# Both layer norms and the residual sum of three token chunks computed inside the attention stage

## The chip, the cores and the metric

The kernel runs on one core of a Trainium2 chip. The time is device microseconds of one execution of the whole program; several executions give a median. A core has a matrix engine (PE, TensorE; its weight loads are listed as PEld), a vector engine (DVE, VectorE), a scalar engine (ACT, ScalarE), GpSimd (POOL) and SP, which here only issues DMAs. Each engine runs its own instruction list in order and waits on semaphores that the others count up.

## The reference, cut to what matters

The model is four layers over 8 sequences of 256 tokens with 256 features (2048 tokens, held as 16 tiles of 128 tokens). The part that the change touches:

```python
x = L0_attn_hidden_states
x = x + _layernorm(_L0_attn_ref(_layernorm(x), w_qkv, b_qkv, w_proj, b_proj))   # y = the attention's output
rows = _layernorm(x)                                                            # what the experts read
x = x + _layernorm(_L0_ffn_ref(rows, router_w, ...))                            # 64 experts, 4 per token
...                                                                             # a scan layer, a feed-forward layer

def _layernorm(x, axis=-1, eps=1e-05):
    m = jnp.mean(x, axis=axis, keepdims=True)
    v = jnp.var(x, axis=axis, keepdims=True)
    return (x - m) / jnp.sqrt(v + eps)
```

Attention has 16 heads of 16 features, a causal mask and a linear position bias. The router computes 64 logits for each token from `rows`, takes the best four experts, and each token's row is written into a slot of each of its four experts.

## The kernel before

The program is a row of stages with a barrier between them. Two matter here.

**Attention** (`stage_attention`, some 82 to 225 us of the span) goes over 16 *units*; a unit is 8 heads of one sequence, so two units make a sequence. All engines loop over a head counter `i`; head `i` lies in unit `i // 8`. For each head PE computes the scores of the head 16 places further on (L529, L530, into one of three banks `ps`) for the maxima that DVE takes (`maxima`, L636 and L638), and then the turned scores of the head itself (L541 to L546, into one of two banks `pst`), of which ACT takes the exponential (`weigh`, L615). The third bank rule is what couples DVE to PE: PE may write scores `n` only once the maxima of `n - 3` are out. The second couples ACT: PE may write turned scores `n` only once the exponential of `n - 2` is out. At the second head of every unit (`i % 8 == 1`) PE does three more things in this order: `turn` (L573), which needs the maxima of a whole unit; `values` (L560), the product with the values of the unit before; and in even units from the fourth on `project` (L583) for a whole sequence. ACT hands the turned maxima over (`hand_over`, L609), POOL splits them into three short rows (L510 to L513), SP writes these into the stack that the turned scores of the next unit but one loop step read (`place`, L484). DVE inverts the sums and normalises (L647, L651), and in even units adds the projection's bias (`add`, L656): that is `y`. In units 4 to 10 SP also issues one block of zeros each (1 MB of `slots_in`, from `blank`, L2617); 16 blocks are needed in all before tokens may be scattered.

**Routing** (`stage_route`, 225 to 381 us) takes the statistics of `y` (`statistics`, L1020 to L1031 on DVE; one over the deviation on POOL, `deviations`, L813 and L814), scales `y` on ACT (L955), adds it to `x` on DVE (`add`, L1036), takes the statistics of `x`, and lets ACT write the normalised `rows` (L955), in four chunks of four tiles. PE turns `rows` (L855), ACT and DVE keep high and low parts (L960, L1042), PE computes the router's logits (`score`, L869), DVE chooses four experts for each token (`choose`, L1048 to L1057), PE counts and ranks (L876 to L887), DVE works out the slot numbers (`tables`, `find_slots`, L1069 to L1121), and POOL scatters the rows with 64 indirect DMAs, 16 for each chunk (L842). POOL also splits the weights of the shared expert (`split`, L819 and L822), and after the scores PE, ACT and DVE run the shared expert's eight steps (L917, L1002, L1137, L1006, L1141) for the first two chunks. The stage ends when the last scatter has landed and the last product of that expert is stored (L995). The other nine blocks of zeros are issued at its start.

Of the kernel before, what the change touches and what calls it, by code (L numbers as in the profile page):

```python
# [13 lines left out]
P = 128  # L14
# [401 lines left out]
LAST_ADD = (UNITS + 2) * HALF + AT_ADD  # L416

# [12 lines left out]
FILL_FIRST, FILL_AT = 7, 4  # L430


def stage_attention(chip, vpad, qk_dram, stack, consts, y, ident, fill, ins):
# [9 lines left out]
    with ExitStack() as ctx:  # L443
# [23 lines left out]
        projected, y_ready = chip.sem("projected"), chip.sem("y_ready")  # L467

# [3 lines left out]
        with nc.Block() as block:  # L472
# [25 lines left out]
            def _(pool):  # L498
# [7 lines left out]
                for u in range(UNITS):  # L506
                    pool.wait_ge(shift_out, u + 1)
                    if u:
# [5 lines left out]
                                            ).then_inc(max_split, 1)  # L514

# [88 lines left out]
            def _(act):  # L604
# [13 lines left out]
                for i in range(-LEAD * HALF, STEPS + HALF):  # L618
                    n = i + LEAD * HALF
                    if 0 <= i < STEPS:  # L620
                        weigh(i)
                    if n % HALF == AT_BLOCK and 0 < n // HALF <= UNITS:
                        hand_over(n // HALF - 1)

            @block.vector
            def _(dve):
# [32 lines left out]

                dve.wait_ge(loaded, 6 * 16)  # L660
# [18 lines left out]
NORM_ORDER = [(0, 0), (0, 1), (1, 0), (1, 1), (0, 2), (0, 3), (1, 2), (1, 3)]  # L679
# [17 lines left out]
def stage_moe(chip, front, spare, x, xh, xl, y, ident, xs, xs_clear, fill, ys, t, ins):  # L697
    with ExitStack() as room:
        sb, _ = chip.memory(room)
        rows = sb("rows", [P, NT, D])  # L700
        stage_route(chip, x, rows, xh, xl, y, ident, xs, xs_clear, fill, t, ins)
# [7 lines left out]
def stage_route(chip, x, rows, xh, xl, y, ident, xs, xs_clear, fill, t, ins):  # L709
# [10 lines left out]
    with ExitStack() as ctx:  # L720
# [25 lines left out]
        stats = sb("stats", [P, 2, NT, 6])  # L746
        small = sb("small", [P, 5, TPC])
        power = sb("power", [P, TPC])
        negmean, var, rstd, shift = (sb(n, [P, 2, NT]) for n in ("negmean", "var", "rstd", "shift"))
# [23 lines left out]
        var_ready, rstd_ready, y_scaled = chip.sem("var_ready"), chip.sem("rstd_ready"), chip.sem("y_scaled")  # L773
# [16 lines left out]
        def normed(kind, g):  # L790
            return NORM_ORDER.index((kind, g)) + 1

        with nc.Block() as block:
# [10 lines left out]
            def _(pool):  # L804
# [3 lines left out]
                link(nc.gpsimd.memset(power[:], -0.5))  # L808
                pool.wait_ge(none_set, 1)

                def deviations(kind, g):
                    pool.wait_ge(var_ready, normed(kind, g))
                    link(nc.gpsimd.tensor_tensor(rstd[:, kind, tiles(g)], var[:, kind, tiles(g)], power[:], ALU.pow))  # L813
                    nc.gpsimd.tensor_tensor(shift[:, kind, tiles(g)], negmean[:, kind, tiles(g)],  # L814
                                            rstd[:, kind, tiles(g)], ALU.mult).then_inc(rstd_ready, 1)
# [9 lines left out]
                for g in range(2):  # L825
                    deviations(OF_Y, g)
                for g in range(2):
                    deviations(OF_X, g)
                for g in range(2, NCH):
                    deviations(OF_Y, g)  # L830
                split(0)
                deviations(OF_X, 2)
                split(1)
                deviations(OF_X, 3)
                split(2)
                split(3)
# [10 lines left out]
            def _(pe):  # L847
                def turn(g):
                    for b in (2 * g, 2 * g + 1):
                        pe.wait_ge(xn_ready, b + 1)  # L850
# [46 lines left out]

                pe.wait_ge(split_done, 2)
                turn(0)
# [5 lines left out]
                place_chunk(1)  # L905
                turn(3)
                score(2)
# [45 lines left out]
            def _(act):  # L953
                def scaled(dst, src, kind, i):
# [60 lines left out]
            def _(dve):  # L1015
# [128 lines left out]
                for g in range(2):  # L1144
                    statistics(y, OF_Y, g)
# [1606 lines left out]
```

## Time and profile before

| | |
|---|---|
| time of three executions | 1388.35, 1390.89, 1393.96 us; median 1390.89 |
| span of the profiled execution | 1388.8 us (its own device time is not listed apart; the median lies 2.1 us above the span) |
| busy share of the span | PE 84%, PEld 70%, DVE 62%, ACT 45%, POOL 27% |
| attention | 82.0 to 225.1 us |
| routing | 225.1 to 381.5 us; first scatter at 277.0, last begun at 366.2 |

The profile is of one execution. A row of a timeline gives the start, the length, the engine, the line, the written and the read tiles with their shapes, and a count when several equal instructions are merged; the bracket is the idle time of the engine ahead of it and what released it. Times of different engines can be laid side by side, since all are counted from the span's start. The granted clock of TensorE is 1.00 (2.4 GHz) through the middle of attention and about 0.5 (1.2 GHz) through the first half of routing.

### The profile page before, as it was taken

The numbers are of one execution on the slowest core, as the hardware profiler recorded it, in microseconds if no ns is written. First come the engines' busy times: TensorE is split into PE (matmuls) and PEld (weight loads), VectorE is DVE, ScalarE is ACT, GpSimd is POOL, SyncE is SP. The second block draws the span as 40 slices with busy tenths as digits, with TensorE's granted clock in tenths as the row PEclk, the third lists the DMA queues.
The fourth block names the chain that finished last, engine by engine and source line by source line (L and its number), as shares of the span: only waits on it lengthen the run. The fifth ranks groups of instructions, "written<-read, shape, count | busy, mean of one in ns | idle before, by whom it ended". The sixth has DMA issues, their size and how long they took to land. (4 is left out here: it accounts for less than half of the span.)

```text
span 1388.8 us, 25315 instructions
## 1 busy us (share of the span) xinstructions
PE 1168.4 (84%) x9088; PEld 974.9 (70%) x9088; DVE 863.8 (62%) x2165; ACT 618.7 (45%) x1415; POOL 370.3 (27%) x467
## 2 busy tenths in 40 slices
PE   6669994635689998767779999999999999997886
PEld 5537762634588986545648888888888888886775
DVE  6468876945546665577456666566666666663464
ACT  5434543302133443446644554545455445552564
POOL 3321112576400446572024005001400240000110
PEclk9879997556789998877799999999999999999998
DMA  7725724322199874353243233223342332222001
GB/s 172 182 78 159 229 66 164 161 103 83 57 397 417 290 254 138 91 155 122 89 113 108 82 94 122 77 84 99 115 137 85 107 107 80 81 62 80 1 16 46
DMA packets 77529, 177.21 MB, mean 128 GB/s; under 512 B 12566, under 2 KB 26134, under 8 KB 74710
## 3 DMA queue, kind: packets, MB, share of 16 engines
q1 hardware_dynamic: 71132, 158.54, 34.7%
q0 software_dynamic: 6272, 17.05, 4.0%
q8 instruction: 73, 1.20, 0.3%
q14 instruction: 52, 0.43, 0.1%
HBM read 114.26 MB, written 61.08 MB: 126 GB/s over the span
## 5 line engine op out<-in xcount | busy, mean ns | idle before, releaser
L2195 ACT ACTIVATE decay<-masked,negcum 128x128 f32<-128x128 f32 x512 | 164.1, 391 | 240.7 <-issue 156.1
L2300 DVE COPY cT<-pcT 128x512 f32<-128x512 f32 x128 | 88.4, 690 | 175.7 <-PE pcT L2119 175.7
L2130 PEld LDWEIGHTS pcb<-cT,bT 128*128 128x128 f32 x1024 | 134.4, 191 | 10.6
L2130 PE MATMUL pcb<-cT,bT 128*128 128x128 f32 x1024 | 135.3, 275 | 0.0
L2057 POOL TENSOR_TENSOR wh<-wraw,none 128x512 fp32r<-128x512 f32 x32 | 34.2, 1070 | 318.9 <-DMA wraw<-in_w_bc 225.4
L2119 PE MATMUL pbT<-xh,wh 128*128 128x512 f32 x256 | 111.9, 437 | 1.3 <-POOL wl L2060 1.3
L2259 DVE TENSOR_TENSOR mixT<-pcb,decay 128x512 f32<-128x512 f32 x128 | 88.5, 691 | 22.9 <-PE pcb L2130 22.6
L2119 PE MATMUL pcT<-xh,wl 128*128 128x512 f32 x256 | 100.6, 393 | 0.0
L2119 PE MATMUL pbT<-xl,wh 128*128 128x512 f32 x256 | 100.1, 391 | 0.0
L2119 PE MATMUL pbT<-xh,wl 128*128 128x512 f32 x256 | 100.0, 390 | 0.0
L2119 PE MATMUL pcT<-xh,wh 128*128 128x512 f32 x256 | 99.7, 390 | 0.0
L2119 PE MATMUL pcT<-xl,wh 128*128 128x512 f32 x256 | 99.6, 389 | 0.0
L2249 DVE TENSOR_TENSOR masked<-cumrow,mask 128x512 f32<-128x512 f32 x128 | 94.1, 736 | 0.0
L615 ACT ACTIVATE probT<-pst 128x384 f32<-128x384 f32 x128 | 60.0, 490 | 68.0 <-PE pst L546 65.3
L2214 ACT ACTIVATE bT<-pbT 128x512 f32<-128x512 f32 x128 | 74.2, 580 | 25.7 <-PE pbT L2119 25.6
L1506 POOL DMA_INDIRECT back<-slots_out,slots x64 | 68.0, 1062 | 28.5 <-issue 28.0
L842 POOL DMA_INDIRECT slots_in<-rows,slots x64 | 65.4, 1022 | 34.0 <-issue 18.9
L1372 DVE TENSOR_TENSOR hT<-gate,pgu 64x512 f32<-64x512 f32 x64 | 44.2, 691 | 31.0 <-ACT gate L1347 30.6
L1240 POOL COPY copies<-weights 128x384 f32 x64 | 32.4, 507 | 114.7 <-issue 95.6
L2119 PEld LDWEIGHTS pbT<-xh,wh 128*128 128x128 f32 x256 | 48.4, 189 | 12.0 <-issue 4.8
L2268 DVE TENSOR_TENSOR cS<-cT,grown 128x256 f32<-128x256 f32 x128 | 56.8, 444 | 0.1
L2119 PEld LDWEIGHTS pbT<-xh,wl 128*128 128x128 f32 x256 | 48.1, 188 | 10.9
(387 smaller groups left out, 3020.1 us busy)
## 6 DMA issues: line engine op xcount, KB each, us to landing
cumrow<-ssm_cum SPq DMA_DIRECT2D x128, 256.0 KB, 3.2
slots_in<-blank SPq DMA_DIRECT2D x16, 1024.0 KB, 10.6
xg<-slots_in SPq DMA_DIRECT2D x32, 512.0 KB, 6.3
slots_out<-spare SPq DMA_DIRECT2D x32, 512.0 KB, 3.8
weights<-in_expert_quads SPq DMA_DIRECT2D x16, 768.0 KB, 10.1
wraw<-in_w_bc SPq DMA_DIRECT2D x32, 256.0 KB, 3.7
qk_parts<-parts SPq DMA_DIRECT2D x32, 192.0 KB, 2.3
stack<-qk_parts SPq DMA_DIRECT2D x32, 192.0 KB, 3.4
```

The costliest lines, as they stand in the source:

```text
L615: nc.scalar.activation(probT[:, n % HELD, :], pst[n % T_BANKS][:, 0:3 * P], ACT.Exp).then_inc(exped, 1)
L842: nc.gpsimd.indirect_dma_start(out=xs[:, :], out_offset=bass.IndirectOffsetOnAxis(slots[:, i, k:k + 1], 0), in_=rows[:, i, :], in_offset=N ...
L1372: last = nc.vector.tensor_tensor(hT[k * FE:(k + 1) * FE, g % 2, :], gate[FE:P, g % 2, :], pgu[g % 2][FE:P, :], ALU.mult)
L1506: nc.gpsimd.indirect_dma_start(out=back[:, i % BACK, k, :], out_offset=None, in_=ys[:, :], in_offset=bass.IndirectOffsetOnAxis(slots[:, i, ...
L2119: last = nc.tensor.matmul(bank[:], w[:, j, col:col + P], a[:, k, c * CHUNK:(c + 1) * CHUNK], start=(m == 0), stop=(m == len(parts) - 1))
L2130: last = nc.tensor.matmul(pcb[n % 2][:, o], bT[:, n % 2, o], cT[:, n % 2, o], start=True, stop=True)
L2195: last = nc.scalar.activation(decay[:, n % 2, o], masked[:, n % 2, o], ACT.Exp, bias=negcum[:, c * TPC + i, head:head + 1])
L2214: nc.scalar.activation(bT[:, n % 2, :], pbT[:], ACT.Copy).then_inc(b_out, 1)
L2249: nc.vector.tensor_tensor(masked[:, n % 2, :].rearrange("p (i l) -> p i l", l=P), cumrow[:, n % CUMS, :].rearrange("p (i l) -> p i l", l=P ...
L2259: nc.vector.tensor_tensor(mixT[:, n % KEEP, :], pcb[n % 2][:], decay[:, n % 2, :], ALU.mult).then_inc(mix_out, 1)
L2268: nc.vector.tensor_tensor(cS[:, n % KEEP, :, :], second, grown[:, n % 2, :, :], ALU.mult).then_inc(c_scaled, 1)
L2300: nc.vector.tensor_copy(cT[:, n % 2, :], pcT[:]).then_inc(c_out, 1)
```

## The change

Of the first three chunks (tiles 0 to 11), the whole of norm, residual sum and second norm is done inside attention, some units after the chunk's `y` is there. Only the last chunk (tiles 12 to 15) stays in the routing stage; of it the statistics of the first two tiles of `y` are taken in attention too. The formulas of the statistics use `bn_aggr` for each tile in place of five small operations for each four tiles. In the attention stage the residual sum runs on POOL, one 128x1024 addition for each chunk. Twelve blocks of zeros are issued in units 4 to 15 in place of seven in units 4 to 10, four instead of nine in routing. In routing PE scores chunk 2 before it turns chunk 3, and DVE chooses for chunk 2 before the low parts of chunk 3. `rows` and the small norm tiles are allocated ahead of attention.

```diff
+EARLY_NORMS = 3
+NORM_SCALE, NORM_SUM, NORM_ROWS = 7, 8, 9
+def measure(nc, link, norms, kind, tiles):
+    for i in tiles:
+        last = nc.vector.bn_aggr(moments[:, kind, i, :], norms["stats"][:, kind, i, :])
+    link(last)
+    nc.vector.tensor_scalar(norms["negmean"][:, kind, part], moments[:, kind, part, 0], -1.0, None, ALU.mult)
+    return nc.vector.tensor_scalar(norms["var"][:, kind, part], moments[:, kind, part, 1], EPS, None, ALU.add)
+def spread(nc, link, norms, kind, tiles):
+    link(nc.gpsimd.tensor_tensor(rstd, norms["var"][:, kind, part], norms["power"][:], ALU.pow))
+    return nc.gpsimd.tensor_tensor(norms["shift"][:, kind, part], norms["negmean"][:, kind, part], rstd, ALU.mult)
+def normal(nc, norms, dst, src, kind, i):
+    return nc.scalar.activation(dst, src, ACT.Identity, bias=norms["shift"][:, kind, i:i + 1],
+                                scale=norms["rstd"][:, kind, i:i + 1])
-FILL_FIRST, FILL_AT = 7, 4
+FILL_FIRST, FILL_AT = 12, 4
@@ attention, gpsimd
-                for u in range(UNITS):
+                for u in range(UNITS + 2):
+                    if u < UNITS:
+                        split(u)
+                    g, at = (u - NORM_SCALE) // 4, (u - NORM_SCALE) % 4
+                    if 0 <= g < EARLY_NORMS and at == 0:
+                        pool.wait_ge(y_measured, g + 1)
+                        spread(nc, norm_step, norms, OF_Y, tiles(g)).then_inc(y_spread, 1)
+                    if 0 <= g < EARLY_NORMS and at == NORM_SUM - NORM_SCALE:
+                        residual(g)          # x = x + y, waits for y_scaled
+                    if 0 <= g < EARLY_NORMS and at == NORM_ROWS - NORM_SCALE:
+                        pool.wait_ge(x_measured, g + 1)
+                        spread(nc, norm_step, norms, OF_X, tiles(g)).then_inc(x_spread, 1)
@@ attention, scalar
+                    g, at = (i // HALF - NORM_SCALE) // 4, (i // HALF - NORM_SCALE) % 4
+                    if 0 <= g < EARLY_NORMS and at == 0 and 2 <= i % HALF < 2 + TPC:
+                        scale_y(g, g * TPC + i % HALF - 2)
+                    if 0 <= g < EARLY_NORMS and at == NORM_ROWS - NORM_SCALE and i % HALF >= HALF - TPC:
+                        fill_row(g, g * TPC + i % HALF - (HALF - TPC))
@@ attention, vector
+                    seq = i // HALF // 2 - 2
+                    if i % (2 * HALF) == AT_ADD + 2 and 0 <= seq < B - 1:
+                        y_statistics(seq)    # two bn_stats; with an odd seq also measure()
+                    g = (i + 1) // HALF // 4 - 2
+                    if 0 <= g < EARLY_NORMS and (i + 1) % (4 * HALF) in (HALF, HALF + 1):
+                        x_statistics(g, (i + 1) % HALF)   # two bn_stats each; the second also measure()
                     u = i // HALF - 2
                     if i % HALF == AT_BLOCK and 0 <= u < UNITS:
@@ routing, vector
-                for g in range(2):
-                    statistics(y, OF_Y, g)
+                statistics(y, OF_Y, last_tiles[TPC // 2:])
...
-                for g in range(2):
-                    add(g)
-                    statistics(x, OF_X, g)
                 set_tables()
-                statistics(y, OF_Y, 2)
                 low_parts(0)
-                statistics(y, OF_Y, 3)
                 low_parts(1)
-                add(2)
-                statistics(x, OF_X, 2)
                 choose(0)
-                add(3)
-                statistics(x, OF_X, 3)
+                add()
+                statistics(x, OF_X, last_tiles)
                 choose(1)
                 low_parts(2)
                 tables(0)
                 find_slots(0)
                 find_slots(1)
+                choose(2)
                 low_parts(3)
-                choose(2)
                 choose(3)
@@ routing, scalar
-                scale_y(0)
-                scale_y(1)
-                normal(0)
                 high_parts(0)
-                normal(1)
-                scale_y(2)
+                scale_y()
                 high_parts(1)
-                scale_y(3)
-                normal(2)
                 high_parts(2)
-                normal(3)
+                fill_rows()
                 high_parts(3)
```

**DVE, units 8 and 9.** DVE's list where the maxima of heads 86 to 88 (loop steps 70 to 72) stand; `ps` are the score banks, `norm_stats` and `norm_moments` the new small tiles. Before, and then after:

```order
L636 ISA masked,highest<-ps_74,reach 128x128
L636 ISA highest 128x1
L638 ISA masked,highest<-ps_74,reach 128x256
L638 ISA highest 128x1
L636 ISA masked,highest<-ps_75,reach 128x128
L636 ISA highest 128x1
L638 ISA masked,highest<-ps_75,reach 128x256
L638 ISA highest 128x1
```

```order
L737 BN_STATS norm_stats<-y 128x6 x2
L708 ISA masked,highest<-ps_74,reach 128x128
L708 ISA highest 128x1
L710 ISA masked,highest<-ps_74,reach 128x256
L710 ISA highest 128x1
L745 BN_STATS norm_stats<-x 128x6 x2
L708 ISA masked,highest<-ps_75,reach 128x128
L708 ISA highest 128x1
L710 ISA masked,highest<-ps_75,reach 128x256
L710 ISA highest 128x1
L745 BN_STATS norm_stats<-x 128x6 x2
L427 BN_AGGR norm_moments<-norm_stats 128x2 x4
```

Three groups of statistics stand between the maxima of three heads that followed one another, the last with four `bn_aggr` and two small scalings behind it.

**DVE, the end of attention.** The last rows ahead of the barrier (`y` of sequences 6 and 7, `rinv` and `oT` of the last unit). Before, and then after:

```order
L656 TENSOR_TENSOR y<-misc,bproj 128x512
L647 RECIPROCAL rinv<-po_80 128x128 x2
L651 TENSOR_TENSOR oT<-po_80,rinv 128x256
L656 TENSOR_TENSOR y<-misc,bproj 128x512
L472 UNCONDITIONAL_BRANCH
```

```order
L728 TENSOR_TENSOR y<-misc,bproj 128x512
L737 BN_STATS norm_stats<-y 128x6 x2
L745 BN_STATS norm_stats<-x 128x6 x4
L427 BN_AGGR norm_moments<-norm_stats 128x2 x4
L430 TENSOR_SCALAR norm_negmean<-norm_moments 128x4
L431 TENSOR_SCALAR norm_var<-norm_moments 128x4
L719 RECIPROCAL rinv<-po_80 128x128 x2
L723 TENSOR_TENSOR oT<-po_80,rinv 128x256
L728 TENSOR_TENSOR y<-misc,bproj 128x512
```

The statistics of two tiles of `y` and of all four tiles of chunk 2 of `x` now stand ahead of the last unit's reciprocals, on which the last projection waits.

**ACT, unit 7.** ACT's list from the handing over of the maxima (`shift`) on; `probT` are the exponentials. Before, and then after:

```order
L609 ACTIVATE shift<-misc 16x128
L615 ACTIVATE probT<-pst_77 128x384
L615 ACTIVATE probT<-pst_78 128x384
L615 ACTIVATE probT<-pst_77 128x384
L615 ACTIVATE probT<-pst_78 128x384
L615 ACTIVATE probT<-pst_77 128x384
```

```order
L666 ACTIVATE shift<-misc 16x128
L672 ACTIVATE probT<-pst_77 128x384
L444 ACTIVATE y<-y,norm_shift,norm_rstd 128x256
L672 ACTIVATE probT<-pst_78 128x384
L444 ACTIVATE y<-y,norm_shift,norm_rstd 128x256
L672 ACTIVATE probT<-pst_77 128x384
L444 ACTIVATE y<-y,norm_shift,norm_rstd 128x256
L672 ACTIVATE probT<-pst_78 128x384
L444 ACTIVATE y<-y,norm_shift,norm_rstd 128x256
```

Four scalings of a tile now alternate with four exponentials.

## Rows read from the trace of the kernel before

**Rows 1.** Busy time of each engine in attention; then the DMA queue of 220:277 (packets, MB, share).

```profile
82.00:225.13 143.13, 132.05 (x1854) 95.43 (x1852) 107.36 (x538) 62.48 (x144) 22.34 (x64) 0.95 0.41 121
...
q1 hardware_dynamic: 2016, 11.24, 50.4%
```

**Rows 2.** Timeline (start, us, engine, line, out<-in, [idle before <-releaser]), ACT, attention.

```profile
129.86 3.02 ACT L615 ACTIVATE probT<-pst 128x384 f32<-128x384 f32 x6 [2.86 <-PE pst L546]
```

**Rows 3.** Timeline, DVE, 123.8 to 129.6, attention.

```profile
123.85 0.69 DVE L656 TENSOR_TENSOR y<-misc,bproj 128x512 f32<-128x512 f32 x1
...
125.56 0.28 DVE L636 CUSTOM_DVE_ANT_0 masked<-ps,reach 128x128 f32<-128x128 f32 x1
...
129.58 0.29 DVE L636 CUSTOM_DVE_ANT_0 masked<-ps,reach 128x128 f32<-128x128 f32 x1
```

**Rows 4.** Timeline, PE, the same two units.

```profile
126.25 0.28 PE L573 MATMUL misc<-ident,highest 128*16 128x128 f32 x1
...
130.70 0.22 PE L529 MATMUL ps<-stack 99*128 99x128 bf16 x1
...
132.58 0.27 PE L541 MATMUL pst<-stack 102*128 102x256 bf16 x1
```

**Rows 5.** Timeline, POOL and then SP's queue, the same unit.

```profile
127.06 0.28 POOL L510 CAST short<-shift 16x128 bf16<-16x128 f32 x1 [7.50 <-ACT shift L609]
...
128.71 2.62 SPq L484 DMA_DIRECT2D stack<-short  x3
```

**Rows 6.** Timeline, DVE, the end of attention.

```profile
218.04 0.69 DVE L656 TENSOR_TENSOR y<-misc,bproj 128x512 f32<-128x512 f32 x1 [5.90 <-PE misc L583]
218.65 1.76 DVE L647 RECIPROCAL rinv<-po 128x128 f32<-128x128 f32 x2
```

**Rows 7.** Timeline of the routing stage: DVE, POOL, DVE, ACT.

```profile
225.46 1.41 DVE L1020 BATCH_NORM_STATS2 stats<-y 128x6 f32<-128x256 f32 x4 [0.32 <-PEq L472]
...
228.06 1.01 POOL L813 TENSOR_TENSOR rstd<-var,power 128x4 f32<-128x4 f32 x1 [2.36 <-DVE var L1031]
...
230.12 0.22 DVE L1147 CAST wh<-wraw 128x128 fp32r<-128x128 f32 x1
...
237.54 2.07 ACT L955 ACTIVATE rows<-x,shift,rstd 128x256 f32<-128x256 f32 x4 [3.86 <-POOL shift L814]
```

**Rows 8.** Timeline, PE and then DVE, scores of chunks 0 and 1.

```profile
244.20 0.40 PE L869 MATMUL pu<-wh,xh 128*128 128x64 f32 x1
...
254.44 1.11 PE L855 MATMUL acc<-ident,rows 128*128 128x128 f32 x4
...
259.63 0.42 DVE L1048 TENSOR_TENSOR ranked<-pg,bias 128x256 f32<-128x256 f32 x1
```

**Rows 9.** Timeline, POOL beside DVE, twice.

```profile
246.37 1.47 POOL L819 TENSOR_TENSOR sh<-sraw,none 128x768 fp32r<-128x768 f32 x1
...
246.47 0.68 DVE L1042 TENSOR_TENSOR xl<-acc,xh 128x512 fp32r<-128x512 f32 x1
...
265.98 1.81 POOL L822 TENSOR_TENSOR sl<-sraw,sh 128x768 fp32r<-128x768 f32 x1
...
266.12 1.72 DVE L1074 TENSOR_SCALAR tiles_i<-count_i 128x64 int32<-128x64 int32 x1
```

**Rows 10.** Timeline of the scatter: POOL, then DVE, then ACT.

```profile
276.99 1.22 POOL L842 DMA_INDIRECT slots_in<-rows,slots  x1 [9.20 <-DVE slots L1121]
...
323.56 0.96 POOL L842 DMA_INDIRECT slots_in<-rows,slots  x1 [5.88 <-DVE slots L1121]
...
366.22 0.96 POOL L842 DMA_INDIRECT slots_in<-rows,slots  x1 [0.30 <-issue]
...
304.49 0.22 DVE L1069 TENSOR_TENSOR table<-table,counts 128x64 f32<-128x64 f32 x1 [14.78 <-remote]
...
319.89 0.60 ACT L1002 ACTIVATE gate<-pg 128x512 f32<-128x512 f32 x1 [52.41 <-remote]
...
380.14 1.09 ACT L995 ACTIVATE y<-acc 128x512 f32<-128x512 f32 x2 [3.26 <-PE acc L927]
```

More of the change, by code:

```diff
@@ L616, in weigh, with scale_y, fill_row @@
                                          ).then_inc(exped, 1)
-                for i in range(-LEAD * HALF, STEPS + HALF):
+                def scale_y(g, i):
+                    act.wait_ge(y_spread, g + 1)
+                    last = normal(nc, norms, y[:, i, :], y[:, i, :], OF_Y, i)
+                    if i % TPC == TPC - 1:
+                        last.then_inc(y_scaled, 1)
+                def fill_row(g, i):
+                    act.wait_ge(x_spread, g + 1)
+                    normal(nc, norms, rows[:, i, :], x[:, i, :], OF_X, i)
+                for i in range(-LEAD * HALF, STEPS + 2 * HALF):
                     n = i + LEAD * HALF
@@ L658, in add, with y_statistics, x_statistics @@
                                             ).then_inc(y_ready, 1)
+                link = linker(dve, norm_chain)
+                def y_statistics(seq):
+                    dve.wait_ge(y_ready, seq + 1)
+                    for i in (2 * seq, 2 * seq + 1):
+                        last = nc.vector.bn_stats(norms["stats"][:, OF_Y, i, :], y[:, i, :])
+                    link(last)
+                    if seq % 2 and seq // 2 < EARLY_NORMS:
+                        measure(nc, link, norms, OF_Y, tiles(seq // 2)).then_inc(y_measured, 1)
+                def x_statistics(g, half):
+                    dve.wait_ge(x_added, g + 1)
+                    for i in tiles(g)[2 * half:2 * half + 2]:
+                        last = nc.vector.bn_stats(norms["stats"][:, OF_X, i, :], x[:, i, :])
+                    link(last)
+                    if half:
+                        measure(nc, link, norms, OF_X, tiles(g)).then_inc(x_measured, 1)
                 dve.wait_ge(loaded, 6 * 16)
@@ L694, with stage_moe @@
 I32 = mybir.dt.int32
[L697 to L701, printed above, removed]
+def stage_moe(chip, front, normed, spare, x, rows, norms, xh, xl, y, ident, xs, xs_clear, fill, ys, t, ins):
+    stage_route(chip, x, rows, norms, xh, xl, y, ident, xs, xs_clear, fill, t, ins)
+    normed.close()
     front.close()
@@ L953, in _ @@
             def _(act):
-                def scaled(dst, src, kind, i):
-                    return nc.scalar.activation(dst, src, ACT.Identity, bias=shift[:, kind, i:i + 1],
-                                                scale=rstd[:, kind, i:i + 1])
                 def high_part(b):
```

118 lines of the change are left out of this document (59 added, 59 removed).

## The prediction

> **What bounds the kernel now.** I read the page's slices, then busy time by stretch, then the timelines of the stages that the change touches. Work leaves the start of routing and enters attention, so I ask of each whether it has room.
>
> Attention has little. PE is busy 132 of 143 us at clock 0.95 [rows 1]. ACT takes six exponentials back to back, 3.02 us or 0.50 each, and idles only ahead of them, 2.86 us, while PE does `values` [rows 2]; in between PE waits for ACT, since there are two banks. DVE takes a head's maxima in 0.555 us. From 125.56, where head 7's begin, it does 7, 8 and 9, then two reciprocals and `oT`, and is at the next head at 129.58: no hole [rows 3]. I call the heads of the even unit shown 0 to 7 and those of the odd unit behind it 8 to 15. PE's turn at 126.25 needs the maxima of head 7, out at 125.56 + 0.56 = 126.12: slack 0.13. PE's scores of head 13 at 130.70 need head 10's maxima, out at 129.58 + 0.56 = 130.14: slack 0.56 [rows 3, 4]. POOL's split begins at 127.06, SP's writes 1.65 later, and the turned scores of the next unit begin at 132.58, 3.87 after SP started [rows 4, 5]; the gap ahead of those scores says that this chain sets them in odd units. Even units have the projection's 2 us as slack.
>
> Routing up to the scatter is one chain through the norms: scores of chunk 0 start at 244.20, 19.1 us after the stage's begin S (225.13), the scatter at 276.99, S + 51.9 [rows 8, 10].
>
> **Attention, part by part.** Prices: a `bn_stats` 0.35 (1.41 for 4), a scaling on ACT 0.52 (2.07 for 4), POOL's `rstd` 1.01, with its `shift` 1.25 [rows 7]. `bn_aggr` is not in the trace. `measure` is four of them and two scalings, against seven small operations that took, with the handing over to POOL, 2.60 - 1.41 = 1.19 us [rows 7]. Below, six pipelined at 0.08 give 0.5; above, aggregates as dear as `bn_stats` give 1.65. I take 0.65, nearest to the small ones.
>
> *Two `bn_stats` of y behind head 6 of an even unit.* Maxima 7 come 0.74 later, slack 0.13: PE's turn and all behind it +0.6. With `measure` (odd sequences) +1.25. Unit 4: 0.6. Units 6 and 10: 1.25 each. Unit 14: nothing, since its maxima are over and DVE waits.
>
> *Four scalings between exponentials, units 7, 11, 15.* ACT is full there, so 4 x 0.52 = 2.0 each, 6.0 in all. The idle 2.86 us can't cover them, because they stand behind heads 2 to 5.
>
> *Units 8 and 9, and 12 and 13.* Statistics behind head 6 (0.74), 7 (0.74) and 8 (0.74 + 0.65). Head 7's maxima are out at 126.87, the turn +0.65. Head 8's end at 128.17, `x_measured` comes at 129.6, head 9's at 130.1, reciprocals and `oT` 132.4, head 10's maxima at 133.0, where PE wanted them at about 131.3: +1.65, +2.3 in all, and PE then goes at DVE's 0.555 and at ACT, which has four `rows` among these heads; `values` would begin 2.9 late. The POOL chain is later still: POOL waits in its list for `x_measured`, so `spread` ends at 130.95, the split that was due at 127.7 ends at 132.6, and 3.87 behind it, at 136.5, PE gets its rows, 3.9 after 132.58. I take 3.8 for each pair of units, 7.6. Behind the waiting POOL instruction stands only this split; it is PE that waits for it.
>
> *The end.* The six `bn_stats` and `measure` stand ahead of the reciprocals that followed the add at once, 218.04 to 218.65 [rows 6]. The last projection waits for these: 6 x 0.35 + 0.1 + 0.65 = 2.85. Chunk 2's four `rows` on ACT lie beside it.
>
> Sum: 0.6 + 2.5 + 6.0 + 7.6 + 2.85 = 19.55 us. With dear aggregates five `measure` on the path add 5; if the stretches overlap better (ACT's delays lying over DVE's), I don't get below 12. So 12 to 25.
>
> *At nothing.* POOL's residual sum is 1.81 x 1024/768 = 2.4 us [rows 9], three times; it waits for ACT's last scaling and ends about when the next split is due, in an even unit. Does it stop DVE? Beside POOL's 1.47 us operation DVE's `xl`, which reads one operand from PSUM, took 0.68 [rows 9], as the add of 512 columns did with POOL idle (0.69, [rows 3]); the maxima read `ps` in the same way: no. The five more blocks of zeros (units 11 to 15) run where little else is loaded; each stands on SP ahead of a `place` that comes a unit later.
>
> **Routing up to the scatter.** `rows` of chunks 0 to 2 are there at S. PE turns chunk 0 at once. Chunk 1 and the scores wait for the split router weights; the cast began at S + 5.0 without a wait [rows 7], so its load was in by then, I take S + 4. Then come two memsets, the tables and four low parts, of which chunk 0's end at S + 6.5, and chunk 1's turning in PE's list holds the scores to S + 7.0. Gain there 19.1 - 7.0 = 12.1. Two chunks of scores take 254.44 - 244.20 = 10.24 [rows 8], until S + 17.3. DVE chose chunk 1 at 259.63, 5.2 behind the scores' end, because the sum and the statistics of chunk 3 lay between [rows 8]; now these follow `choose(0)` and end at S + 18.55, 1.3 behind it: 3.9 more, 16.0.
>
> Against it: three of POOL's four splits now follow the last `spread` (S + 19.8) and run to S + 30, over `tables(0)`, which starts at S + 22.6. DVE is slow beside them: a 64-column operation took 1.72 us, until POOL's of 265.98 ended [rows 9], where one of that width takes 0.22 [rows 10]. One or two slip in between two of POOL's, so I put DVE at a quarter of its pace: over 7.4 us that loses 5.3. Before, the splits ended at 267.8 [rows 9], some 4 us into the tables, and cost about 3: -2. Gain 14.0, scatter at S + 37.9. Bounds: no contention 17, standing still throughout and `measure` dear 11.
>
> The Trainium skill ("SBUF — State Buffer", SBUF: two separate sides) says that the port pair of VectorE and GpSimd is an exclusive lock for the whole instruction, against a VectorE operation with two SBUF inputs or a two-port mode. By that rule DVE would do nothing in the 7.4 us, and the gain would be 12 instead of 14; the trace shows it slipping an operation in between POOL's, so the sum goes by the trace.
>
> The nine blocks of zeros were 9 of the 11.24 MB that kept the queue at 50.4% of 57 us [rows 1], 2.6 us for a MB; four and the shared weights take 14 us, done by S + 17. They bound nothing before (scatter at S + 51.9) and nothing now.
>
> Up to the scatter: +19.55 - 14.0 = +5.5.
>
> **From the scatter on.** The first 32 indirect DMAs run 41 us, POOL then waits 5.88, and the rest ends at 367.2; the stage's last copies end at 381.2, 104.3 after the first scatter [rows 10]. In that time DVE stood 14.78 us and ACT 52.41, both behind PE's signals that by PE's rows were due at 291 and 293, and ACT went on at 319.89 just when the scatter paused [rows 10]. I can't name the cause, and the change doesn't touch it: DVE's and ACT's last work ahead of it stands 13 to 16 us into the scatter as before. I take 104.3 unchanged.
>
> Total: +5.5 on 1390.9, **1396 us**. The sum is made on the profiled span of 1388.8; I set its difference on the median, 2.1 above.
>
> **Rivals.**
> *A, as summed,* 1396; attention's +12 to +25 and the gain of 17 to 11 give bounds of 1386 to 1405. Chance 42%.
> *B, faster: the hold beside the scatter shrinks.* It could, since choosing for chunk 2 now comes earlier and the pause of 5.88 goes when slots are ready. Then only POOL's 64 operations bound it: 90.2 less 5.88, and 2 for landing, 86 in place of 104.3, up to 18 less: 1378; half of it 1387. For it: the PE part ahead ends earlier; against it: two engines were held to the pause, whatever lay ready. 30%.
> *C, slower: the hold lasts longer.* If ACT is freed only when POOL pauses, and DVE has chunk 2's slots ready before that, POOL goes on with 48 instead of 32, 1.27 us each, 20 us more; ACT's eight steps, 61 us from 319.89, then start that much later: +18, 1414, decided by whether slots of chunk 2 are ready before the 32nd DMA. Against it: in the trace DVE was held too. 17%.
> *D, attention costs only 10* because ACT's insertions and DVE's lie over one another: 1387. For it: while ACT holds PE, DVE catches up; against: only units 7 and 8 touch, and the turn waits for DVE before it. 11%.
>
> **How the numbers follow.** About 0.5%, 7 us, can be told from no change: faster is below 1384, slower above 1398. A gives same 27, slower 15; B faster 20, same 10; C slower 17; D faster 4, same 7. So faster 0.24, same 0.44, slower 0.32. The range 1380 to 1411 takes in A, D, most of B and C up to 1411; A's own is 1386 to 1405.
>
> **What would show it.** Attention should last 155 to 168 instead of 143 us; in units 7, 11 and 15 PE waits for ACT over four heads; in units 9 and 13 the turned scores wait for `stack<-short`, some 4 us; the last reciprocals come 3 us behind the add. The scatter should begin 36 to 41 us after the stage's start, and the stage end some 104 us after that. Wrong: attention growing by under 10, or the scatter-to-end stretch shifted by over 8 us.

## The result, and the profile after

The changed kernel took 1402.6 us (median of 7 runs, 1395.9 to 1410.3) against 1391.7 for the kernel before, beside which it ran: ratio 1.0071, 95% interval 1.0049 to 1.0094, so 0.7% slower, some 10 us by the ratio and 11 by the medians. The forecast was 1396, in the range 1380 to 1411. The profiled execution has a span of 1399.5 us against 1388.8.

I cut both traces at the same three places: ScalarE's first copy of `shift`, the start S of the routing stage, and the stage's last copy of `y`. First the busy times of attention's whole, then of stretches of it (us, busy us of PE, PEld, DVE, ACT and POOL, PEclk, DMA share, GB/s), and then the DMA queue of the routing stage up to the scatter:

```profile
86.00:251.92 165.92, 141.06 (x1853) 99.93 (x1852) 121.04 (x598) 73.42 (x168) 36.33 (x79) 0.90 0.42 136
...
178.00:187.00 9.00, 7.44 (x93) 5.62 (x83) 6.46 (x38) 3.80 (x8) 1.41 (x4) 1.00 0.81 271
187.00:190.50 3.50, 3.50 (x41) 2.15 (x45) 3.09 (x11) 0.27 (x1) 1.94 (x6) 0.53 0.51 209
...
214.70:221.20 6.50, 5.75 (x59) 3.31 (x61) 3.11 (x11) 2.74 (x7) 1.40 (x4) 0.50 0.41 166
...
246.00:251.50 5.50, 3.78 (x8) 2.52 (x8) 1.59 (x4) 2.07 (x4) 0.53 (x2) 0.50 0.00 0
...
q1 hardware_dynamic: 1296, 6.00, 36.8%
```

Attention has as many matmuls as in [rows 1], but they are busy 9 us longer, and the granted clock is 0.90 for 0.95. Both kernels enter the stage at the lower of TensorE's two levels, 1.2 GHz (until 91.6 us before and 98.4 after; up to unit 4 the difference in time is 0.3 us). Behind that the changed kernel ran at the lower level in four stretches; three of them stand here, the fourth is 235 to 238.5. The timeline of PE (start, us, line, out<-in, wait and releaser) shows the first of them and the last, and then the last projection of the kernel before:

```profile
186.93 0.28 PE L630 MATMUL misc<-ident,highest 128*16 128x128 f32 x1 [1.27 <-DVE highest L710]
187.13 1.08 PE L617 MATMUL po<-probT,vpad 128*32 128x256 f32 x8
...
247.41 3.78 PE L640 MATMUL misc<-wproj,oT 128*128 128x256 f32 x8 [5.97 <-DVE oT L723]
...
220.92 3.49 PE L583 MATMUL misc<-wproj,oT 128*128 128x256 f32 x8 [2.92 <-DVE oT L651]
```

The turn waited 1.27 us for VectorE's maxima, and the eight matmuls of `values` behind it took 1.08 us; in a unit at 2.4 GHz the same row says 0.64. The last projection waited 5.97 us and took 3.78; the ones before it took 1.99. The kernel before had its last projection slow too, 3.49 us behind a wait of 2.92: that was its only stretch at 1.2 GHz between 91.6 us and the end of attention. So the changed kernel's longer wait costs 3 us there, and the clock only 0.3 more than before. Why it waited stands in VectorE's timeline, which answers to [rows 6]:

```profile
241.48 0.69 DVE L728 TENSOR_TENSOR y<-misc,bproj 128x512 f32<-128x512 f32 x1 [8.85 <-PE misc L640]
242.21 0.75 DVE L737 BATCH_NORM_STATS2 norm_stats<-y 128x6 f32<-128x256 f32 x2
243.00 1.54 DVE L745 BATCH_NORM_STATS2 norm_stats<-x 128x6 f32<-128x256 f32 x4
244.57 0.38 DVE L427 BATCH_NORM_AGGREGATE norm_moments<-norm_stats 128x2 f32<-128x6 f32 x4
244.99 0.17 DVE L430 TENSOR_SCALAR norm_negmean<-norm_moments 128x4 f32<-128x4 f32 x1
245.06 0.16 DVE L431 TENSOR_SCALAR norm_var<-norm_moments 128x4 f32<-128x4 f32 x1
245.13 1.76 DVE L719 RECIPROCAL rinv<-po 128x128 f32<-128x128 f32 x2
```

From the add to the reciprocals it is 3.65 us, 0.61 before. In the routing stage (S = 251.92) VectorE and GpSimd answer to [rows 9], first DVE's, then POOL's:

```profile
277.17 1.72 DVE L1134 TENSOR_SCALAR tiles_i<-count_i 128x64 int32<-128x64 int32 x1
278.92 1.39 DVE L1135 TENSOR_SCALAR table<-tiles_i 128x64 f32<-128x64 int32 x1
280.35 1.84 DVE L1136 TENSOR_SCALAR table<-table 128x64 f32<-128x64 f32 x1
...
277.03 1.81 POOL L907 TENSOR_TENSOR sl<-sraw,sh 128x768 fp32r<-128x768 f32 x1
278.80 1.47 POOL L904 TENSOR_TENSOR sh<-sraw,none 128x768 fp32r<-128x768 f32 x1
280.34 1.80 POOL L907 TENSOR_TENSOR sl<-sraw,sh 128x768 fp32r<-128x768 f32 x1
```

Each of these DVE operations begins just behind or with a POOL operation and ends with it, within 0.05 us. The scatter, as in [rows 10] POOL, DVE and then ACT:

```profile
290.88 1.22 POOL L920 DMA_INDIRECT slots_in<-rows,slots  x1 [8.74 <-DVE slots L1181]
...
337.98 0.96 POOL L920 DMA_INDIRECT slots_in<-rows,slots  x1 [6.58 <-DVE slots L1181]
...
380.94 0.96 POOL L920 DMA_INDIRECT slots_in<-rows,slots  x1 [0.30 <-issue]
...
324.25 0.22 DVE L1129 TENSOR_TENSOR table<-table,counts 128x64 f32<-128x64 f32 x1 [17.73 <-remote]
...
336.18 0.60 ACT L1071 ACTIVATE gate<-pg 128x512 f32<-128x512 f32 x1 [53.80 <-remote]
...
394.24 1.08 ACT L1064 ACTIVATE y<-acc 128x512 f32<-128x512 f32 x2 [2.51 <-PE acc L1006]
```

| | before | after | difference | forecast |
|---|---|---|---|---|
| first `shift` copy | 82.75 | 86.47 | +3.7 | 0 |
| attention, from there to S | 142.4 | 165.5 | +23.1 | +19.55 |
| S to the first scatter | 51.9 | 39.0 | -12.9 | -14.0 |
| first scatter to the last copy's end | 104.2 | 104.4 | +0.2 | 0 |
| the rest | 1007.6 | 1004.2 | -3.4 | 0 |

The first and the last line are not the change's: with the same code ahead of attention the first `shift` copy came between 81.6 and 86.5 us in the traces below (86.34 in e1, whose kernel is the one before but for five transfers in attention), so the trace of before was an early one. In the twelve traces whose T stands in the next table the rest lasted between 998 and 1014 us, with the same code.

### The profile page after: what moved, and what is told of

Same layout as the page of the kernel before. It is cut to its first block and busy times, and to the rows that moved or that the text cites. A ratio compares the mean times of both kernels' runs of the same rounds, so it can differ in the third digit from the quotient of the medians.

```text
span 1399.5 us, 25308 instructions
## 1 busy us (share of the span) xinstructions
PE 1170.5 (84%) x9088; PEld 974.1 (70%) x9088; DVE 857.9 (61%) x2154; ACT 617.8 (44%) x1415; POOL 376.8 (27%) x470
## 5 line engine op out<-in xcount | busy, mean ns | idle before, releaser
L2311 DVE TENSOR_TENSOR mixT<-pcb,decay 128x512 f32<-128x512 f32 x128 | 88.5, 692 | 22.9 <-PE pcb L2182 22.6
L920 POOL DMA_INDIRECT slots_in<-rows,slots x64 | 65.5, 1024 | 34.2 <-issue 18.9
L1424 DVE TENSOR_TENSOR hT<-gate,pgu 64x512 f32<-64x512 f32 x64 | 44.2, 691 | 30.6 <-ACT gate L1399 30.2
```

Of the source, the lines that this page charges most:

```text
L920: nc.gpsimd.indirect_dma_start(out=xs[:, :], out_offset=bass.IndirectOffsetOnAxis(slots[:, i, k:k + 1], 0), in_=rows[:, i, :], in_offset=N ...
L1424: last = nc.vector.tensor_tensor(hT[k * FE:(k + 1) * FE, g % 2, :], gate[FE:P, g % 2, :], pgu[g % 2][FE:P, :], ALU.mult)
L2311: nc.vector.tensor_tensor(mixT[:, n % KEEP, :], pcb[n % 2][:], decay[:, n % 2, :], ALU.mult).then_inc(mix_out, 1)
```

## The experiments

The ratios are to the kernel before in the same series, with 95% intervals. Attention (A), S to the first scatter (R) and the first scatter to the last copy (T) are read from each run's trace in the way above.

| run | A | R | T | ratio |
|---|---|---|---|---|
| before | 142.4 | 51.9 | 104.2 | 1 |
| after | 165.5 | 39.0 | 104.4 | 1.0071 (1.0049 to 1.0094) |
| e1_fill | 142.5 | 51.9 | 109.4 | 1.0006 (0.9991 to 1.0021) |
| e2_act | 157.1 | 39.0 | 106.6 | 1.0047 (1.0030 to 1.0064) |
| e3_dve | 148.7 | 38.8 | 111.0 | 0.9967 (0.9951 to 0.9984) |
| e4_both | 143.9 | 38.9 | 105.4 | 0.9930 (0.9910 to 0.9950) |
| e5_busy | 159.6 | 38.0 | 103.8 | 1.0001 (0.9977 to 1.0024) |
| e6_tail | 139.8 | 38.8 | 103.8 | 0.9899 (0.9861 to 0.9938) |
| e7_tiny | 166.3 | 33.3 | 105.8 | 1.0044 (1.0016 to 1.0072) |
| e8_order | 167.1 | 39.5 | 105.1 | 1.0068 (1.0041 to 1.0095) |
| e9_final_2 | 139.3 | 34.5 | see below | 0.9865 (0.9841 to 0.9889) |
| e10_before_tail_2 | 139.0 | 51.9 | see below | 0.9982 (0.9966 to 0.9997) |
| e11_after_2 | 168.1 | 39.1 | 105.0 | 1.0088 (1.0053 to 1.0122) |
| e12_final_again_2 | 139.5 | 35.2 | 107.1 | 0.9861 (0.9839 to 0.9883) |

T swings by 7 us with nothing changed in it, so one trace's span tells little. A repeats within 0.5 us where the granted clock does (139.8, 139.3 and 139.5 in e6, e9 and e12). R lay between 38.0 and 39.1 with the changed kernel's code for it, and at 34.5 and 35.2 with e9's.

**e1_fill.** The kernel before with the blocks alone:
```diff
-FILL_FIRST, FILL_AT = 7, 4
+FILL_FIRST, FILL_AT = 12, 4
```


> The kernel before with FILL_FIRST at 12: the five more blocks of slots are zeroed in attention and nothing else is changed. Theory (these 5 writes lie in DMA queues that the attention stage leaves half idle): the ratio to the kernel before is 1.000 within 0.002, attention 142.4 us within 0.3, and the routing stage 156.4 within 0.5. Rival (they push the stack loads or the three shift rows back): attention grows by 1 to 3 us, ratio above 1.001. Beside this, a profile of it tells how far the front stage, whose code is the same in all kernels, moves from execution to execution: its first shift copy came at 82.75 us before and at 86.47 after.


A 142.5, R 51.9, ratio 1.0006. The five blocks cost nothing and bring nothing. The routing stage took 161 us, where 156.4 within 0.5 was expected: all of it is T, 5.2 longer in this trace, and the ratio does not show it.

**e2_act.** ScalarE's scalings and fills behind a `shift` copy, four at a time:
```diff
-if ... at == 0 and 2 <= i % HALF < 2 + TPC:
-    scale_y(g, g * TPC + i % HALF - 2)
+if i % HALF == AT_BLOCK:      # units 7, 11, 15; rows in 10, 14 and behind the last
+    for k in tiles(g): scale_y(g, k)
```


> The changed kernel with ScalarE's twelve scalings of y and twelve fills of rows taken from between the exponentials and put, four at a time, right behind a shift copy, where ScalarE idles 2.6 us (y, units 7, 11 and 15) or 4.6 us (rows, units 10 and 14, and behind the last unit). VectorE and GpSimd as in the changed kernel. Theory (each group of four between exponentials held TensorE 2.0 us, and the granted clock fell once more behind it): attention 165.5 - 6.0 - up to 3 = 156 to 159.5 us, total 1393 to 1397, ratio to the kernel before 1.001 to 1.004. Rival (the excess over my sum, 3.5 us, comes from VectorE's statistics alone): attention only 6 us shorter at most, TensorE still at 1.2 GHz behind the turn of units 11 and 15. Second rival (contention of the engines, wherever the work stands): attention stays at 163 us or more.


A 157.1, 8.4 us less, more than the first rival allowed. The ratio is a little above the 1.004 expected. Unit 11 lost nearly all that it had gained (7.33 us from one `shift` copy to the next, 10.40 in the changed kernel, 7.15 before). Unit 7 stayed as long, 9.01 for 8.72, for a reason that its PE timeline shows beside unit 11's:

```profile
147.39 0.28 PE L632 MATMUL misc<-ident,highest 128*16 128x128 f32 x1 [1.27 <-DVE highest L714]
147.59 0.77 PE L619 MATMUL po<-probT,vpad 128*32 128x256 f32 x8
148.12 1.10 PE L619 MATMUL po<-probT,ones 128*32 128x256 f32 x8
...
185.99 0.28 PE L632 MATMUL misc<-ident,highest 128*16 128x128 f32 x1 [1.27 <-DVE highest L714]
186.19 0.64 PE L619 MATMUL po<-probT,vpad 128*32 128x256 f32 x8
```

The same wait of 1.27 us is there twice; the clock fell behind the first and not behind the second, in the changed kernel the other way round. So the clock is a term of its own, and which unit pays it is not fixed.

**e3_dve.** VectorE's statistics behind the normalisation of even units, GpSimd's steps behind them; the scalings still between exponentials (units 9, 13 and 15). With them the fills of `rows` went behind the last exponential, which the text below does not name:
```diff
+Y_STATS_DUE = {6: (0,), 8: (1,), 10: (2,), 12: (3,), 14: (4,)}   # at i % HALF == AT_BLOCK
+X_STATS_DUE = {14: (0,), 15: (1,), 16: (2,)}
+POOL_DUE = {9: (("y", 0),), 10: (("sum", 0),), 13: (("y", 1),), 14: (("sum", 1),),
+            16: (("x", 0), ("y", 2), ("x", 1)), 17: (("sum", 2), ("x", 2))}
```


> The changed kernel with VectorE's statistics taken from between the maxima and put behind the normalisation of even units, where VectorE idles 2.2 us (seq 5 and the sums' statistics where there are no maxima any more), and with GpSimd's small steps and sums behind them in that order; the scalings of y stay between exponentials (units 9, 13 and 15). Theory: what goes is 0.6 (unit 4), 1.2 and 1.1 (units 6, 10), 3.1 and 3.4 (units 8-9, 12-13), 3.0 and 1.8 in the tail: 14.2; what stays is three times 2.0 and perhaps the clock behind them: attention 149 to 152 us, total 1386 to 1389, ratio to the kernel before 0.996 to 0.999. Rival (contention): attention 160 us or more.


A 148.7, 16.8 us less than the changed kernel: the statistics' places were the greater part. The fills have little part in it: e2 moved them too, and its units 9 and 13 are 0.1 and 0.4 us shorter than the changed kernel's. The units with scalings take 8.54 and 8.45 us for the 7.15 and 7.07 of before: 1.4 each, not 2.0.

**e4_both.** e3 with the scalings behind a `shift` copy (units 9, 13, 15; the fills of `rows` behind the last exponential).

> Both moves together: no added instruction of VectorE or ScalarE stands where the trace of before has it busy on the path. Theory: attention within 3 us of the 142.4 of before, the granted clock as before, total 1402.6 - 20 to 23 = 1380 to 1383, ratio to the kernel before 0.992 to 0.995; the routing stage keeps its 143.7. Rival (the added 30 us of work on three engines slows the stage through ports and memory, wherever it stands): attention 148 us or more, ratio 0.997 or more.


A 143.9, the granted clock 1.00 from 120 to 222 us. The same instructions, all of them, cost 1.5 us instead of 23.1 (0.3 of the 1.5 is the last projection, 3.78 us for 3.49), so the rival of contention wherever they stand falls. Ratio 0.9930.

**e5_busy.** The changed kernel with TensorE given idle work where it waits (66 transposes in the trace; the 71 of the text below is a miscount):
```diff
+def busy(count):
+    pe.wait_ge(shift_out, issued["turns"]); pe.wait_ge(y_ready, issued["projects"])
+    for _ in range(count): nc.tensor.transpose(misc[:, 0:P], ident[:], ident[:])
```


> The changed kernel with TensorE given something to do where its trace shows it waiting for VectorE, ScalarE or the shift rows: 71 transposes of the identity into the bank of the projections, 3 or 5 ahead of a turn (units whose turn waited 0.72 or 1.27 us), 5 ahead of the scores that waited 1.33, 2 or 3 ahead of the shift rows, one beside each of four scalings, 3 ahead of the last `values` and 25 ahead of the last projection, which waited 5.97. Nothing is computed with them and no wait is taken away. Theory (3.5 us of attention's 23.1 come of the granted clock at 0.5 behind such waits, and more than that if all are counted: 1.7 in the unit from 187, about 2.5 from 215 to 221, 1.4 from 235, 1.8 in the last projection, 7.4 together): attention 158 to 161 us instead of 165.5, the eight `values` rows from 187 at 0.64 for 1.08, the last projection at 1.99 for 3.78, total 1395 to 1399. Rival (the clock falls for another reason, and idling has nothing to do with it): attention 165 us or more, total 1402 to 1405.


PE's timeline, the same place as at 186.93 in the changed kernel, and the last projection:

```profile
182.38 0.71 PE L587 MATMUL misc<-ident 128*128 128x128 f32 x5
183.82 0.28 PE L644 MATMUL misc<-ident,highest 128*16 128x128 f32 x1 [0.72 <-DVE highest L733]
184.03 0.64 PE L628 MATMUL po<-probT,vpad 128*32 128x256 f32 x8
...
233.32 2.92 PE L587 MATMUL misc<-ident 128*128 128x128 f32 x25 [0.87 <-DVE y L751]
238.41 3.68 PE L657 MATMUL misc<-wproj,oT 128*128 128x256 f32 x8 [2.17 <-DVE oT L746]
```

A 159.6, 5.9 us less, by adding work and removing none; every `values` ran at 0.64. The last projection did not profit: the 25 transposes took 2.92 us, ended 2.17 early, and it ran at 1.2 GHz (3.68). The theory holds but for that term, and of its 1.8 us the kernel before had 1.5 already (3.49 us for 1.99). Where the clock of the changed kernel had not fallen, the units of both traces last equally long, so the transposes themselves cost nothing. The ratio fell by more than A, 0.0070 or 9.7 us. e8 below ran in the same series with the same attention and took 10.3 us more than e5; its A is 7.5 us longer and its R 1.5.

**e6_tail.** e4 with the last reciprocals ahead of the add of sequence 6, and its statistics ahead of the add of sequence 7:
```diff
+if u == UNITS - 2:
+    for half in range(2): invert(UNITS - 1, half)
+    normalise(UNITS - 1)
 add(u // 2 - 1)
```


> Both moves, and in the tail of attention the last two reciprocals and the last normalisation stand ahead of the add of seq 6, and the statistics of seq 6 ahead of the add of seq 7 (in e4 they stood behind it). In e4 the last `values` ended at 218.9, the add of seq 6 came at 220.99, the reciprocals at 221.60, the last projection at 223.87, at 1.2 GHz (3.78 us). Theory: the reciprocals start at 218.9, the normalisation ends at 221.1, the add of seq 6 at 221.7, the last projection starts 2.2 us earlier, right behind PE's previous one, and so runs at 2.4 GHz (1.99 us), and 0.6 us of statistics go: attention 143.9 - 2.2 - 1.8 - 0.6 = 139.3 us, total 1375 to 1377, ratio to the kernel before 0.989 to 0.991. Rival (the clock falls all the same): attention 141 us, total 1377 to 1379.

```profile
216.48 1.77 DVE L727 RECIPROCAL rinv<-po 128x128 f32<-128x128 f32 x2 [0.43 <-PE po L623]
...
219.45 1.97 PE L646 MATMUL misc<-wproj,oT 128*128 128x256 f32 x8 [1.12 <-DVE y L736]
```

A 139.8 (139.3 expected). With 1.12 us of waiting in place of 2.92 (e4 and the kernel before) the last projection ran at 2.4 GHz.

**e7_tiny.** Three of the four splits on GpSimd shrunk to 16 columns; the shared expert takes block 0's weights for all.
```diff
+cols = WBLK if s == 0 else 16
```


> The changed kernel without three of the four splits of the shared weights on GpSimd: blocks 1 to 3 are split in 16 columns only and the shared expert takes block 0's weights for all four, so its output is not the reference's. It asks what the splits cost VectorE, whose four 64-column operations beside them took 1.50, 1.72, 1.39 and 1.84 us for 0.21 each. Theory (the splits held them back 5.6 us, and the first scatter waits for VectorE): the first scatter 33.4 us behind the start of the routing stage instead of 38.96, total 5.6 us less than the changed kernel if the scatter sets the end: 1397, ratio to the kernel before 1.002 to 1.005. Rival (the operations were waiting for something else, the counts of TensorE or the limits of the tables): the first scatter stays at 38 us or later.

```profile
274.98 0.20 DVE L1135 TENSOR_SCALAR tiles_i<-count_i 128x64 int32<-128x64 int32 x1
...
284.33 1.22 POOL L921 DMA_INDIRECT slots_in<-rows,slots  x1 [11.13 <-DVE slots L1182]
```

`tiles_i` takes 0.20 us for 1.72, and R is 33.3, 5.6 less (33.4 expected).

**e8_order.** The routing stage's late order as before.
```diff
-choose(2); low_parts(3)        # VectorE; TensorE: score(2); turn(3)
+low_parts(3); choose(2)        # turn(3); score(2)
```


> The changed kernel with the routing stage's late order as before: `low_parts(3)` ahead of `choose(2)` on VectorE and `turn(3)` ahead of `score(2)` on TensorE. Theory (both stand behind the slots of chunks 0 and 1, so the first scatter does not see them, and the next chunk's slots are wanted 47 us after it): the first scatter at 38.96 us within 0.2, total within 1 us of the changed kernel's 1402.6, ratio to the kernel before 1.006 to 1.009. Rival (the order makes the pause between chunks 1 and 2 of the scatter, 6.58 us after for 5.88 before): the pause changes by over 1 us and the total with it.


R 39.5, 0.3 more than I allowed, the pause in the scatter 6.12 us, ratio 1.0068: the new order is worth nothing that can be told. A was 167.1 here and 166.3 in e7, both with the changed kernel's attention: in e7 the unit from 175.71 took 12.34 us at a mean clock of 0.85, where it took 10.22 in the trace of after.

**e9_final_2.** e6 with the splits out of VectorE's way:
```diff
+for s in range(SHARED):        # ScalarE, behind high_parts(1)
+    nc.scalar.activation(sh[:, s, :], sraw[:, s, :], ACT.Copy).then_inc(s_half, 1)
 # GpSimd: only the subtractions, all four ahead of deviations(OF_X)
```


> e6 with the splits of the shared weights out of VectorE's way: ScalarE copies the four high parts where it idles 10.4 us (230.5 to 240.9 in e6), and GpSimd does its four subtractions, 1.85 us each, ahead of the last `spread` instead of behind it. Theory (what e7 showed with the splits left out, 5.7 us, is to be had with the splits in): they end 19 us behind the start of the stage, ahead of `tables(0)` at 22.8; the first scatter 33 to 34 us behind the start instead of 38.7, total 1373.3 - 5 = 1368, ratio to the kernel before 0.985 to 0.988. Rival (the splits slow whatever VectorE does beside them, so the loss moves to `choose(0)`, the sum and the statistics of x): the first scatter at 36 us or later, ratio 0.989 or more.

```profile
236.50 2.84 DVE L1110 TENSOR_TENSOR x<-x,y 128x1024 f32<-128x1024 f32 x1
...
232.69 8.32 POOL L919 TENSOR_TENSOR sl<-sraw,sh 128x768 fp32r<-128x768 f32 x4 [8.59 <-ACT sh L1070]
```

R 34.5 for 38.8 (33 to 34 expected). The rival has a part in it: the sum of x, 1.22 us in e6, took 2.84 beside the four subtractions. Ratio 0.9865; the interval overlaps e6's, so that the split's new place pays is shown by R and not by the ratio.

**e10_before_tail_2.** The kernel before with e6's tail only.

> The kernel before with nothing but e6's tail: the last two reciprocals and the last normalisation stand ahead of the add of seq 6. It tells how much of e6's ratio has nothing to do with the norms. Theory: the reciprocals start at 216.0 instead of 218.65 (the last `values` ended there), the last projection starts 2.2 to 2.7 us earlier; attention 142.4 - 2.4 = 140.0 us, ratio to the kernel before 0.998 to 0.999. Rival (the add of seq 6 and the last projection's bank are what the end waits for): attention 142.4, ratio 1.000.


A 139.0, 3.4 less (2.4 expected); ratio 0.9982. Of e6's 1% a fifth has nothing to do with the norms. The last projection waited 1.11 us and took 1.97, for 2.92 and 3.49 before, so 1.5 of the 3.4 us are the clock's; I had not counted them. Against this kernel the norms in e6's places cost attention 0.8 us.

In these two runs T was another: ScalarE's wait beside the scatter (the hold), 46 to 57 us `remote` in all other traces, was gone. The kernel before, of which this series has no trace, took 1368.5 us in it for 1387 to 1392 in the others. e10 against [rows 10], ACT and the last indirect DMA:

```profile
290.46 0.60 ACT L1006 ACTIVATE gate<-pg 128x512 f32<-128x512 f32 x1 [25.73 <-PE pg L921]
...
358.43 0.96 POOL L846 DMA_INDIRECT slots_in<-rows,slots  x1 [0.30 <-issue]
```

**e11_after_2 and e12_final_again_2.** The changed kernel and e9's in one series.

> The changed kernel itself again, beside e12, since in the runs of e9 and e10 ScalarE's wait beside the scatter (52 to 55 us 'remote' in eight traces) was gone, in the kernel before too, which then took 1368.5 us instead of 1387 to 1391. Theory (the hold belongs to the chip on which a program runs, and the scatter's pace and ScalarE's chain behind it are the same in both kernels, so the change is worth the same with it and without): ratio to the kernel before 1.005 to 1.010 whichever of the two the traces show, attention 165 to 168 us, the first scatter 39 us behind the stage's start. Rival (the hold hid part of the routing gain, or gave it): without the hold the ratio is under 1.003 or over 1.012.

> e9's kernel once more, in one series with the changed kernel and the kernel before. Theory: attention 139.5 us, the first scatter 34.4 us behind the stage's start, against 165.5 to 168 and 39: 31 us less than e11, ratio to the kernel before 0.984 to 0.989, and e12 over e11 0.978. Rival (e9's ratio of 0.9865 was that of a chip without the hold, and with it the splits on ScalarE cost something beside the scatter): ratio 0.990 or more where the traces show the hold.


The hold was back (ACT 53.65 and 47.14 us `remote`). A was 168.1 and 139.5, R 39.1 and 35.2 (39 and 34.4 expected). The kernel before took 1390.8 us, the changed one 1402.9 (1.0088) and e9's kernel 1373.3 (0.9861, for 0.9865 without the hold; over the changed kernel 0.979, 0.978 expected). The rival falls for e9's kernel; for the changed kernel I have no run without the hold, so that half stays open. The theory that the hold belongs to the chip is not borne out: by the record e1 to e4, which had it, and e9 and e10, which had not, all ran on chip 0, and e5 to e8 and e11 and e12, which had it, on chips 3 and 4.

## Why the prediction was right where it was, and what it missed

The forecast of 1396 lies 6.6 us under the median. In the profiled traces attention and routing up to the scatter made +10.2 us where I had +5.5: 3.5 of the difference are attention's and 1.1 routing's. By the prediction's own threshold of 1398 the result is slower, which it gave 0.32, less than the 0.44 of "same". With e5's trace, in which no `values` ran slow, the placements and the clock come apart (us from one `shift` copy to the next, less before's):

| | forecast | e5 | after |
|---|---|---|---|
| unit 4, statistics | 0.6 | 0.8 | 0.8 |
| units 6 and 10, statistics and `measure` | 2.5 | 2.3 | 2.3 |
| units 7 and 11, scalings | 4.0 | 3.1 | 4.8 |
| units 8-9 and 12-13 | 7.6 | 6.3 | 6.5 |
| the rest to S (unit 15 and the end) | 4.85 | 4.4 | 8.5 |

- **Right: statistics beside the maxima delay the turn by their own length**, 0.13 us of slack aside. `bn_aggr`, which I had to bound, took 0.38 us for four, `measure` 0.57 for the 0.65 taken.
- **Four scalings between exponentials cost 1.5 us, not 2.0.** ScalarE was not quite full in these four heads; e3 says 1.4 each.
- **Units 8-9 and 12-13: the size near, the mechanism partly not.** I had TensorE wait for the shift rows behind GpSimd's `spread`. GpSimd was held as I said (its split came at 171.03, behind a `spread` at 169.80), but TensorE's wait for `stack<-short` was 0.51 and 0.75 us, where I had 4. It had lost 1.32 us to VectorE's maxima ahead of that, and the rows were there 2.9 us behind SP's first, for 3.87 in [rows 4, 5].
- **The end: the 3 us of statistics ahead of the reciprocals were there** (3.65 less 0.61).
- **The step that failed: the sum had no term for TensorE's clock.** I priced the waits that the change puts in and took every matmul behind them at the duration of before. After 1.3 to 6 us of waiting, or several short waits in a row, the matmuls ran at 1.2 GHz, in an unlike place in each execution. Four executions of that attention took 165.5, 166.3, 167.1 and 168.1 us, and e5's 159.6: the clock is 5.9 to 8.5 us of it. The last projection adds 0.2 to that, since it ran at 1.2 GHz before too (3.49 us; 3.68 in e5, 3.78 after).
- **That the sum came so near is luck.** In the profiled trace the clock is 6.1 of the 23.1 us, so the placements alone are 17.0 where I had 19.55. Two errors of opposite sign, 2.5 too much for the placements and 6.1 left out, left only 3.5.
- **Routing: right step by step.** Scores from S + 7.45 (7.0 forecast), `choose(1)` at S + 18.8 (18.55), `tables(0)` at S + 23.0 (22.6), the splits to S + 30.2, 5.6 us lost beside them (5.3; e7 measured 5.6), the scatter at S + 38.96 (37.9), the shared weights and the blocks no bound. VectorE waited 2.84 us for the loads and began its cast at S + 4.6, where I had 4. The 5.3 was itself a slip: a quarter of its pace over 7.4 us loses 5.55. The Trainium skill's rule ("SBUF — State Buffer", SBUF: two separate sides), that the port of VectorE and GpSimd is an exclusive lock for a whole instruction, fits the held operations better than my "a quarter of its pace" does: each ended with GpSimd's. It holds per operation: those that slip in between take their usual 0.2.
- **From the scatter on: unchanged, as forecast.** Rivals B and C, 47% together, hung on a change of the hold. It did not change with the kernel; e9 and e10 show it come and go with the series. Where it was gone, the scatter was bound as B had it: its 64 DMAs took 85 us from the first to the end of the last, where B's sum has 84 and 2 for landing. D had its direction right (the placements cost less than their sum), not its size.

## What to carry to other kernels

Work moved into a busy stage costs by its place: the same 26 `bn_stats`, 24 scalings and 3 sums cost 23 us between the maxima and the exponentials (17 in waits, 6 by the clock) and 1.5 us in the idle time that each engine has once per unit, so first list, from the timeline, where each engine idles in one period of the loop, and put the work there. A wait added to TensorE is priced with the matmuls behind it at both levels of its clock. Look also at what the clock costs the kernel before: its last projection was slow already, and moving three instructions won 3.4 us. And a stretch that swings by 7 us with the same code, as T does here, is to be compared in several executions before a difference of 5 us in it is read as the change's.

## What the runs showed of the hardware that I had not expected

- Adding 66 useless transposes where TensorE waited made the kernel faster: ratio 1.0001 for 1.0071, attention 159.6 us for 165.5 to 168.1.
- The hold beside the scatter, 52.41 us of ScalarE and 14.78 of VectorE in [rows 10], is not the program's alone: with the same code from the scatter on (e10), one series had none of it, and the kernel before was 19 to 23 us faster there. What holds the engines in the other series stays open.
- GpSimd stopped only some of VectorE's operations: a sum of two operands in SBUF (1024 columns, 2.84 us for 1.22) and 64-column scalings from SBUF to SBUF (1.39 to 1.84 for 0.2). The maxima, which read PSUM, kept their 0.555 us beside GpSimd's 2.4 us sums. GpSimd was held as well: beside that sum its four subtractions took 8.32 us, 2.08 each, for 1.80 to 1.89 in the changed kernel.

The version that beats both, e9's kernel, takes 0.9861 of the kernel before and 1373.3 us for 1402.9 of the changed one in the same series.
